# Attention with a running state, and a feed-forward layer: x transposed by TensorE in fp32 instead of in two fp16 parts by DMA

## The chip, the cores and the metric

The kernel runs on one core of a Trainium2 chip. Its time is the device time of one execution in microseconds (us); the median of the runs counts. A core has TensorE (PE; its weight loads are shown as PEld), VectorE (DVE), ScalarE (ACT), GpSimd (POOL), SyncE (SP, which here only issues DMAs) and 16 DMA engines. Each engine goes through its own list of instructions in order, and waits for the others by semaphores. SBUF is the memory of 128 partitions that they work on, PSUM the banks that TensorE writes.

## The reference

```python
x = L0_attn_x                                   # (4, 2048, 512) fp32
xn = _layernorm(x, axis=-1)                     # no gain or shift, eps 1e-5
# attention, 64 heads of width 8, heads(y): (4*64, 2048, 8)
q = heads(xn @ Wq.T + bq); k = heads(xn @ Wk.T + bk); v = heads(xn @ Wv.T + bv)
be = jnp.exp(beta)
q = jax.nn.softmax(be * q, axis=-1); k = jax.nn.softmax(be * k, axis=-1)
kv = jnp.cumsum(jnp.einsum('zsD,zsd->zsDd', k, v), axis=1)
kn = jnp.cumsum(k, axis=1)
num = jnp.einsum('zsD,zsDd->zsd', q, kv)
den = jnp.sum(q * kn, axis=-1, keepdims=True)
att = unheads(num / den) @ Wo.T + bo
# feed-forward: input rounded to fp8 (e4m3), clipped to +-448
x_q = jnp.clip(xn / input_scale, -448, 448).astype(jnp.float8_e4m3fn).astype(xn.dtype) * input_scale
ffn = jnp.einsum('bsi,oi->bso', x_q, weight_fp8 * weight_scale) + bias
return x + att + ffn
```

## The kernel before

The work goes in 64 steps. A step takes 32 tokens of each of the 4 sequences, 128 rows, one per partition. The cumulative sums are kept as a running state (st_run); inside a step the scores of q and k under a triangular mask (att) do the rest. Step i's tokens pass through the engines over several rounds of the loop: round i of `body` projects tokens i, does the attention of tokens i-1 and the output of tokens i-2, and gets x of tokens i+1 ready. Each engine has its own `body(i)`, written out by hand; that order is all that sets the order of the work. TensorE has its 64 rounds unrolled in the path that runs here (lines 1043 to 1045), the others loop over four.

fp32 accuracy of the projections comes from fp16 parts: every weight is held as w_hi + w_lo, and x as a high and a low part, so that `project` (L858) makes 12 matmuls of 512 columns for each of k, q and v. Before, the layer-normed x (xn, `normalise`, L597) is split in its natural layout, rows in partitions: ScalarE writes the high part (`high_input`, L450), GpSimd the low part (`low_input`, L388), and SP turns both with one DMA transpose into xT (`turn_x`, L311). ScalarE also scales xn into y. The rounding to fp8 is done by hand: VectorE makes from y's exponent a number y_magic (`magic`, L606), GpSimd adds and subtracts it (`rounding`, L396), VectorE clips (`quantise`, L617), and a second DMA transpose makes xq (`turn_xq`, L318). GpSimd also computes the reciprocal root of the variance by twelve small operations for two steps at once, in even rounds (`root`, L365).

TensorE's round is: k projection; scores and state of the first half (L888, L905); transpose of the attention output into the bank t_ps (L931); q projection; scores and state of the second half; feed-forward (L963); output projection (L872 to L876); q against the state (L985, 128 small matmuls that wait for masked_ready, stseqs_ready and qheads_ready); v projection; att against v (L1004, 128 small matmuls). masked_ready is given by VectorE's `mask_state` (L635; st_masked in the profile).

## Time and profile before

| | |
|---|---|
| median of 3 runs | 1386.97 us (1383.36 to 1387.37) |
| profiled execution | 1375.45 us, its span 1373.7 us |
| mean granted TensorE clock | 0.967 |
| TensorE busy | 1224.7 us, 89% |
| VectorE busy | 1024.7 us, 75% |
| ScalarE busy | 577.5 us, 42% |
| GpSimd busy | 321.5 us, 23% |
| DMA | 106.01 MB, 181142 packets; 120160 of them under 512 B |

Busy time is the time in which an instruction of the engine runs. The page's fourth part follows the work that ended last back to what released it: 86% of that chain is TensorE, 8% "issue", which is time in which the engine waited for nothing that the profile shows. In the rows below a matmul is named by what it writes and reads (vo_ps<-w_hi,al); "idle before" in brackets is how long its engine had nothing to do, and what ended that.

### The profile page before, as it was taken

The page shows a single profiled execution, that of the slowest core. Times are in us where ns is not written, and L with a number is a line of the kernel's source. Part 1 is how long each engine was busy: PE and PEld are TensorE (multiplying, and loading weights), DVE is VectorE, ACT ScalarE, POOL GpSimd, SP SyncE. Part 2 cuts the span into 40 slices and gives each one's busy share as a digit, 9 for nine tenths or more (in the row PEclk, how much of TensorE's full clock was granted, in tenths as well). Part 3 has the DMA queues.
Part 4 walks back from the last instruction along what each step waited for, and adds up shares of the span by engine and source line. Part 5 has one row for each costly group of instructions (what it writes and reads, how often), then busy time and mean ns, then how long its engine had stood idle before and what let it go on. Part 6 is the DMA issues. An engine that isn't in the chain of part 4 may idle for free.

```text
span 1373.7 us, 81313 instructions
## 1 busy us (share of the span) xinstructions
PE 1224.7 (89%) x36322; PEld 731.5 (53%) x36322; DVE 1024.7 (75%) x2031; ACT 577.5 (42%) x1049; POOL 321.5 (23%) x590
## 2 busy tenths in 40 slices
PE   1569999998999999999999899999999999999995
PEld 1335555555555555555555555555555555555653
DVE  4667778877777887778777777877777877778872
ACT  1534344444444444444444344344344444344431
POOL 3132222222222222222222222221222222122210
PEclk8789999999999999999999999999999999999998
DMA  8022232323323333333333333233233333323321
GB/s 223 10 67 65 75 84 75 82 76 79 75 73 83 70 85 76 81 74 85 76 75 77 76 80 71 77 79 69 76 86 66 76 86 77 75 77 76 69 65 42
DMA packets 181142, 106.01 MB, mean 77 GB/s; under 512 B 120160, under 2 KB 153056, under 8 KB 180832
## 3 DMA queue, kind: packets, MB, share of 16 engines
q1 hardware_dynamic: 180112, 99.79, 30.3%
q8 instruction: 289, 4.73, 1.5%
q10 hardware_dynamic: 720, 1.31, 0.6%
q14 instruction: 21, 0.17, 0.1%
HBM read 40.20 MB, written 16.78 MB: 41 GB/s over the span
## 4 chain that ended last, share of the span: by engine, by line
PE 86%; issue 8%; DVE 2%; DMA 1%; SPq 1%; POOL 0%; ACT 0%; POOLq 0%; DVEq 0%; ACTq 0%
PE s_ps L888 10%; PE a_ps L985 7%; PE a_ps L1004 6%; PE a_ps L905 6%; PE k_ps L861 5%; PE vo_ps L861 5%; PE vo_ps L963 5%; PE vo_ps L863 4%; PE k_ps L865 4%; PE vo_ps L865 4%; PE k_ps L863 4%; PE vo_ps L872 4%; PE vo_ps L874 4%; PE vo_ps L876 4%; PE q_ps L863 4%
## 5 line engine op out<-in xcount | busy, mean ns | idle before, releaser
L507 ACT ACTIVATE q_heads<-qT,cst 128x512 f32<-128x512 f32 x256 | 164.0, 711 | 88.1 <-DVE qT L753 88.1
L400 POOL TENSOR_TENSOR y_sum<-y,y_magic 128x512 f32<-128x512 f32 x64 | 81.4, 1272 | 450.3 <-DVE y_magic L614 450.3
L659 DVE TENSOR_TENSOR att<-s_ps,cst 128x512 f32<-128x512 f32 x256 | 163.8, 681 | 2.1 <-PE s_ps L888 2.1
L393 POOL TENSOR_TENSOR x_split<-xn,x_split 128x512 f16<-128x512 f32 x64 | 74.0, 1157 | 370.6 <-ACT x_split L455 363.4
L498 ACT ACTIVATE q_e<-q_shift,q_exp_scale 128x512 f32<-128x512 f32 x64 | 46.2, 722 | 252.0 <-DVE q_shift L632 252.0
L888 PE MATMUL s_ps<-q_heads,kT 32*32 32x128 f32 x8192 | 148.3, 272 | 2.1 <-issue 1.2
L888 PEld LDWEIGHTS s_ps<-q_heads,kT 32*32 32x32 f32 x8192 | 113.6, 103 | 56.3 <-issue 56.3
L985 PE MATMUL a_ps<-st_seqs,q_heads 128*32 128x36 f32 x8192 | 99.3, 201 | 35.6 <-issue 33.9
L712 DVE TENSOR_TENSOR vp<-vo_ps,vp 128x512 f32<-128x512 f32 x64 | 44.3, 692 | 109.1 <-PE vo_ps L865 109.1
L985 PEld LDWEIGHTS a_ps<-st_seqs,q_heads 128*32 128x32 f32 x8192 | 89.1, 109 | 68.4 <-issue 66.1
L905 PE MATMUL a_ps<-vp,k_e 32*32 32x36 f32 x8064 | 115.0, 198 | 6.4 <-issue 6.3
L861 PE MATMUL k_ps<-w_hi,xT 128*128 128x512 f16 x256 | 101.4, 396 | 19.0 <-DMA xT<-x_split 11.7
L863 PE MATMUL vo_ps<-w_lo,xT 128*128 128x512 f16 x256 | 102.0, 398 | 9.8 <-issue 9.8
L905 PEld LDWEIGHTS a_ps<-vp,k_e 32*32 32x32 f32 x8064 | 101.3, 103 | 11.5 <-issue 8.2
L470 ACT ACTIVATE vo_ps<-bias,out_up 128x512 f32<-128x512 f32 x64 | 44.3, 692 | 148.7 <-DVE vp L712 142.9
L455 ACT ACTIVATE x_split<-xn 128x512 f16<-128x512 f32 x64 | 40.3, 630 | 157.4 <-DVE xn L603 157.4
L1004 PE MATMUL a_ps<-v_groups,att 128*32 128x36 f32 x8192 | 89.3, 199 | 18.5 <-issue 14.9
L865 PE MATMUL k_ps<-w_hi,xT 128*128 128x512 f16 x256 | 100.2, 391 | 5.7 <-issue 5.6
L1004 PEld LDWEIGHTS a_ps<-v_groups,att 128*32 128x32 f32 x8192 | 79.6, 109 | 45.4 <-issue 45.1
L861 PE MATMUL vo_ps<-w_hi,xT 128*128 128x512 f16 x256 | 101.7, 397 | 0.0
L865 PE MATMUL vo_ps<-w_hi,xT 128*128 128x512 f16 x256 | 101.5, 396 | 0.0
L863 PE MATMUL k_ps<-w_lo,xT 128*128 128x512 f16 x256 | 100.4, 392 | 0.0
(136 smaller groups left out, 2450.4 us busy)
## 6 DMA issues: line engine op xcount, KB each, us to landing
v_groups<-vp SPq DMA_DIRECT2D x1024, 18.0 KB, 2.4
x_in<-L_attn_x SPq DMA_DIRECT2D x64, 256.0 KB
x_res<-L_attn_x SPq DMA_DIRECT2D x64, 256.0 KB
out<-o_sb SPq DMA_DIRECT2D x64, 256.0 KB
w_own<-L_attn_Wk SPq DMA_DIRECT2D x1, 1024.0 KB, 11.4
w_own<-L_attn_Wq SPq DMA_DIRECT2D x1, 1024.0 KB, 13.5
w_own<-L_attn_Wv SPq DMA_DIRECT2D x1, 1024.0 KB, 15.2
att<-L_ffn_weight_fp SPq DMA_DIRECT2D x1, 1024.0 KB, 16.9
```

Of the source, the lines that this page charges most:

```text
L393: gp.tensor_tensor(x_split[:, 1, :], xn[:, :], x_split[:, 0, :], ALU.subtract)\
L400: gp.tensor_tensor(y_sum[:, :], y[:, :], y_magic[:, :], ALU.add).then_inc(ysum_ready, 1)
L507: last = sc.activation(q_heads[:, i.parity, :, j, :], qT[:, :, :], ACT.Copy, scale=head_mask[:, j:j + 1])
L659: v.tensor_tensor(att[:, c, :, :, :].rearrange("p g j s -> p (g j) s"), s_ps[:, DM * (c % 2):DM * (c % 2 + 1)].rearrange("p (h s) -> p h s ...
L861: mm(bank[:, :], xT[:, t.parity, 0, c, :], w_hi[:, m, c, :], start=(c == 0 and not seeded), stop=False, skip_group_check=seeded)
L863: mm(bank[:, :], xT[:, t.parity, 0, c, :], w_lo[:, m, c, :], start=False, stop=False, skip_group_check=seeded)
L865: last = mm(bank[:, :], xT[:, t.parity, 1, c, :], w_hi[:, m, c, :], start=False, stop=(c == KC - 1), skip_group_check=seeded)
L888: last = mm(s_ps[TOK * gl:TOK * (gl + 1), DM * n + P * gq:DM * n + P * (gq + 1)], kT[rows, t.parity, GL * gq + gl, :], q_heads[rows, t.par ...
L905: last = mm(a_ps[rows, col:col + J * VW], k_e[rows, t.parity, TOK * g:TOK * (g + 1)], vp[rows, t.parity, v_head(g):v_head(g) + J, :], star ...
L963: last = mm(vo_ps[:, :], xq[:, t.slot, c, :], w_hi[:, MF, c, :], start=False, stop=False, skip_group_check=True)
L985: mm(a_ps[TOK * j:TOK * (j + 1), a_col(g):a_col(g) + GW], q_heads[:, t.parity, g, j, :], st_seqs[:, t.parity, g, :, :], start=(g % (G // 2 ...
L1004: last = mm(groups[TOK * j:TOK * (j + 1), b], att[:, b, gq, j, :], v_groups[:, t.parity, :, b, gq, j, :], start=False, stop=True, skip_gro ...
```

## The change

xn is turned as it is, in fp32: TensorE transposes its four 128x128 blocks into the bank t_ps (`input_transpose`). ScalarE then copies the high part out of PSUM as fp16, already transposed (xh), and the scaled y as well; VectorE subtracts to get the low part (xl). The rounding chain works on the transposed y, so `quantise` writes xq directly. Both DMA transposes are gone from SP, and the subtraction from GpSimd. t_ps is now shared by the transposed x and the transposed attention output, which adds waits between their writers and readers. The steps move: in ScalarE's round `high_input` stands behind q_heads instead of at the start, in VectorE's `low_input` and `magic` stand ahead of scale_values at the end, and GpSimd does `root` ahead of `rounding`.

In the diff, context that says nothing is left out.

```diff
@@ -170,9 +170,8 @@
         xn = sb("xn", [P, DM])
-        x_split = sb("x_split", [P, 2, DM], F16)
-        xT = sb("xT", [P, 2, 2, KC, P], F16)
-        xq_rows = sb("xq_rows", [P, DM], F16)
+        xh = sb("xh", [P, 2, KC, P], F16)
+        xl = sb("xl", [P, 2, KC, P], F16)
         y = sb("y", [P, DM])
@@ -308,26 +306,9 @@
-            def turn_x(t):
-                sp.wait_ge(xl_ready, (t + 1).n)
-                if t.after(2):
-                    sp.wait_ge(v_done, (t - 1).n)
-                sp.dma_start_transpose(xT[:, t.parity].rearrange("p h c s -> p (h c) s"),
-                                       x_split[:, :, :].rearrange("p h d -> p (h d)")).then_inc(x_turned, 16)
-
-            def turn_xq(t):
-                sp.wait_ge(xq_ready, (t + 1).n)
-                if t.after(SLOTS):
-                    sp.wait_ge(f_done, (t - SLOTS + 1).n)
-                sp.dma_start_transpose(xq[:, t.slot, :, :], xq_rows[:, :]).then_inc(xq_turned, 16)
-
             def body(i):
...
                     move_v(i - 1)
-                if (i + 1).exists():
-                    turn_x(i + 1)
-                if i.exists():
-                    turn_xq(i)
                 if (i + SLOTS).exists():
@@ -385,14 +365,6 @@
-            def low_input(t):
-
-                pool.wait_ge(xh_ready, (t + 1).n)
-                if t.after(1):
-                    pool.wait_ge(x_turned, t.n * 16)
-                gp.tensor_tensor(x_split[:, 1, :], xn[:, :], x_split[:, 0, :], ALU.subtract)\
-                    .then_inc(xl_ready, 1)
-
             def rounding(t):
@@ -405,16 +377,14 @@
             def body(i):
-                if (i + 1).exists():
-                    low_input(i + 1)
-                    rounding(i + 1)
                 if i.parity == 0 and (i + PAIR).exists():
                     root(i + PAIR)
+                if (i + 1).exists():
+                    rounding(i + 1)
...
             root(Step(0, 0))
-            low_input(Step(0, 0))
             rounding(Step(0, 0))
@@ -449,14 +419,14 @@
-                act.wait_ge(xn_ready, (t + 1).n)
-                if t.after(1):
-                    act.wait_ge(x_turned, t.n * 16)
-                sc.activation(x_split[:, 0, :], xn[:, :], ACT.Copy).then_inc(xh_ready, 1)
+                act.wait_ge(xT_done, (t + 1).n)
+                if t.after(2):
+                    act.wait_ge(v_done, (t - 1).n)
+                sc.activation(flat(xh[:, t.parity]), t_ps[:, :], ACT.Copy).then_inc(xh_ready, 1)
                 if t.after(1):
...
                     act.wait_ge(magic_ready, t.n)
-                sc.activation(y[:, :], xn[:, :], ACT.Copy, scale=in_inv[:, :]).then_inc(y_ready, 1)
+                sc.activation(y[:, :], t_ps[:, :], ACT.Copy, scale=in_inv[:, :]).then_inc(y_ready, 1)
@@ -469,8 +439,6 @@
                         .then_inc(oseed_ready, 1)
-                if (i + 1).exists():
-                    high_input(i + 1)
                 if i.exists():
@@ -507,6 +475,8 @@
                     last.then_inc(qheads_ready, 1)
+                if (i + 1).exists():
+                    high_input(i + 1)
                 t = i - 1
@@ -598,14 +568,21 @@
                 if t.after(1):
-                    dve.wait_ge(xl_ready, t.n)
-                    dve.wait_ge(y_ready, t.n)
+                    dve.wait_ge(xT_done, t.n)
                 v.tensor_scalar(xn[:, :], x_in[:, t.slot, :], mv[:, t.slot, 0:1],
...
+            def low_input(t):
+
+                dve.wait_ge(xh_ready, (t + 1).n)
+                dve.wait_ge(y_ready, (t + 1).n)
+                if t.after(2):
+                    dve.wait_ge(v_done, (t - 1).n)
+                v.tensor_tensor(flat(xl[:, t.parity]), t_ps[:, :], flat(xh[:, t.parity]), ALU.subtract)\
+                    .then_inc(xl_ready, 1)
+
             def magic(t):
...
-                dve.wait_ge(y_ready, (t + 1).n)
                 v.tensor_scalar(y_exp[:, :].bitcast(I32), y[:, :].bitcast(I32), EXPONENT, None,
@@ -617,9 +594,9 @@
                 dve.wait_ge(yround_ready, (t + 1).n)
-                if t.after(1):
-                    dve.wait_ge(xq_turned, t.n * 16)
-                v.tensor_scalar(xq_rows[:, :], y_round[:, :], FP8_MAX, -FP8_MAX, ALU.min, ALU.max)\
+                if t.after(SLOTS):
+                    dve.wait_ge(f_done, (t - SLOTS + 1).n)
+                v.tensor_scalar(flat(xq[:, t.slot]), y_round[:, :], FP8_MAX, -FP8_MAX, ALU.min, ALU.max)\
                     .then_inc(xq_ready, 1)
@@ -741,8 +718,6 @@
                     shift(i, q_ps, q_done, q_max, qmax_ready, q_shift, qshift_ready, qe_ready)
-                if (i + 1).exists():
-                    magic(i + 1)
                 if t.exists():
@@ -765,6 +740,9 @@
                     variances(i + PAIR)
+                if (i + 1).exists():
+                    low_input(i + 1)
+                    magic(i + 1)
                 if i.exists():
@@ -809,6 +787,7 @@
             largest(MQ)
+            low_input(Step(0, 0))
             magic(Step(0, 0))
@@ -858,11 +837,11 @@
                 for c in range(KC):
-                    mm(bank[:, :], xT[:, t.parity, 0, c, :], w_hi[:, m, c, :], start=(c == 0 and not seeded),
+                    mm(bank[:, :], xh[:, t.parity, c, :], w_hi[:, m, c, :], start=(c == 0 and not seeded),
                        stop=False, skip_group_check=seeded)
-                    mm(bank[:, :], xT[:, t.parity, 0, c, :], w_lo[:, m, c, :], start=False, stop=False,
+                    mm(bank[:, :], xh[:, t.parity, c, :], w_lo[:, m, c, :], start=False, stop=False,
                        skip_group_check=seeded)
-                    last = mm(bank[:, :], xT[:, t.parity, 1, c, :], w_hi[:, m, c, :], start=False,
+                    last = mm(bank[:, :], xl[:, t.parity, c, :], w_hi[:, m, c, :], start=False,
                               stop=(c == KC - 1), skip_group_check=seeded)
@@ -889,6 +868,13 @@
                 last.then_inc(scores_done, 1)
+
+            def input_transpose(t):
+
+                pe.wait_ge(xn_ready, (t + 1).n)
+                for c in range(KC):
+                    last = transpose(t_ps[:, P * c:P * (c + 1)], xn[:, P * c:P * (c + 1)], ident)
+                last.then_inc(xT_done, 1)
@@ -908,7 +894,8 @@
                 if i.exists():
-                    pe.wait_ge(x_turned, (i + 1).n * 16)
+                    pe.wait_ge(xh_ready, (i + 1).n)
+                    pe.wait_ge(xl_ready, (i + 1).n)
                     pe.wait_ge(kseed_ready, (i + 1).n)
@@ -923,16 +910,15 @@
                     pe.wait_ge(an_ready, (t + 1).n)
-                    if t.after(1):
-                        pe.wait_ge(al_ready, t.n)
-                    else:
-                        pe.wait_ge(bvl_ready, 1)
+                    if i.exists():
+                        pe.wait_ge(y_ready, (i + 1).n)
                     for b in range(SEQS):
...
                     pe.wait_ge(bias_ready, 3)
+                    pe.wait_ge(y_ready, (i + 1).n)
                     for j in range(J):
@@ -957,7 +943,7 @@
                 if t.exists():
-                    pe.wait_ge(xq_turned, (t + 1).n * 16)
+                    pe.wait_ge(xq_ready, (t + 1).n)
                     pe.wait_ge(oseed_ready, (t + 1).n)
@@ -971,6 +957,13 @@
                     project_out(rest=True).then_inc(o_done, 1)
+                if (i + 1).exists():
+                    if fold:
+                        pe.wait_ge(bvl_ready, 1)
+                    else:
+                        pe.wait_ge(xl_ready, (i + 1).n)
+                        pe.wait_ge(y_ready, (i + 1).n)
+                    input_transpose(i + 1)
                 t = i - 1
@@ -1029,6 +1022,7 @@
             pe.wait_ge(c_loaded, 16)
+            input_transpose(Step(0, 0))
             for m in (MK, MQ, MV):
...
             pe.wait_ge(wl_ready, qkv_chunks)
```

TensorE, before, in the middle of the run: the end of the output projection, then L985 (a_ps<-st_seqs,q_heads), then v.

```order
L872 MATMUL vo_ps<-w_hi,ah 128x512
L874 MATMUL vo_ps<-w_lo,ah 128x512
L876 MATMUL vo_ps<-w_hi,al 128x512
L985 MATMUL a_ps<-st_seqs,q_heads 32x36 [waits stseqs_ready,masked_ready,qheads_ready]
L985 MATMUL a_ps<-st_seqs,q_heads 32x36 x63
```

The same place in the changed kernel, whose line numbers are lower (L855 was L876, L978 was L985).

```order
L851 MATMUL vo_ps<-w_hi,ah 128x512
L853 MATMUL vo_ps<-w_lo,ah 128x512
L855 MATMUL vo_ps<-w_hi,al 128x512
L876 MATMUL t_ps<-cst,xn 128x128 [waits xn_ready,y_ready,xl_ready]
L876 MATMUL t_ps<-cst,xn 128x128 x3
L978 MATMUL a_ps<-st_seqs,q_heads 32x36 [waits stseqs_ready,masked_ready,qheads_ready]
L978 MATMUL a_ps<-st_seqs,q_heads 32x36 x63
```

Four transposes of xn stand between the output projection and L985.

GpSimd, before, in an even round: rounding, then root, whose first three operations stand here.

```order
L393 TENSOR_TENSOR x_split<-xn,x_split 128x512 [waits x_turned,xh_ready]
L400 TENSOR_TENSOR y_sum<-y,y_magic 128x512 [waits magic_ready,y_ready]
L404 TENSOR_TENSOR y_round<-y_sum,y_magic 128x512 [waits xq_ready,ysum_ready]
L378 TENSOR_TENSOR newton<-guess 128x2 [waits xn_ready,guess_ready]
L380 TENSOR_TENSOR newton<-newton,minus_half 128x2 [waits newton_steps]
L382 TENSOR_TENSOR newton<-newton,three_halves 128x2 [waits newton_steps]
```

In the changed kernel, the end of root and what follows it in the same round.

```order
L358 TENSOR_TENSOR newton<-newton 128x2 [waits newton_steps]
L360 TENSOR_TENSOR newton<-newton,minus_half 128x2 [waits newton_steps]
L362 TENSOR_TENSOR newton<-newton,three_halves 128x2 [waits newton_steps]
L364 TENSOR_TENSOR rstd<-newton 128x2 [waits newton_steps]
L372 TENSOR_TENSOR y_sum<-y,y_magic 128x512 [waits magic_ready,y_ready]
L376 TENSOR_TENSOR y_round<-y_sum,y_magic 128x512 [waits xq_ready,ysum_ready]
```

The subtraction is gone, and y_sum and y_round stand behind root. On VectorE two pieces move; the changed kernel's end of a round shows where they now are.

```order
L547 BN_STATS stats<-x_in 128x6 [waits x_loaded0]
L548 REGISTER_ALU
L550 BN_AGGR mv<-stats 128x2 [waits stats_ready]
L577 REGISTER_ALU [waits mv_ready]
L581 TENSOR_TENSOR xl<-t_ps,xh 128x512 [waits v_done,y_ready,xh_ready]
L586 TENSOR_SCALAR y_exp<-y 128x512
L591 TENSOR_SCALAR y_magic<-y_exp 128x512 [waits yround_ready,yexp_ready]
L689 TENSOR_TENSOR vp<-vo_ps,vp 128x64x8 [waits krec_ready,v_done]
```

Before, vp followed the statistics directly, and y_exp and y_magic stood between q_shift and the second pair of masks.

## Rows read from the trace of the kernel before

**Rows 1.** Page, section 1: busy us, share, instructions

```profile
PE 1224.7 (89%) x36322; PEld 731.5 (53%) x36322; DVE 1024.7 (75%) x2031; ACT 577.5 (42%) x1049; POOL 321.5 (23%) x590
```

**Rows 2.** List of waits of TensorE: us in total, times, longest us

```profile
PE a_ps L985 <- issue: 33.9, 40, 2.9
...
PE a_ps L1004 <- issue: 14.9, 13, 2.5
...
PE k_ps L861 <- DMA xT<-x_split: 11.7, 1, 11.7
```

**Rows 3.** Two steps: stretch, us; PE, PEld, DVE, ACT, POOL busy; clock; DMA share; GB/s

```profile
699.30:718.00 18.70, 18.39 (x569) 11.12 (x570) 15.77 (x33) 8.62 (x17) 5.03 (x10) 1.00 0.28 70
718.00:739.20 21.20, 18.92 (x570) 11.38 (x570) 15.37 (x29) 8.99 (x17) 4.72 (x9) 1.00 0.37 88
```

**Rows 4.** Chain of waits of step A, and its last L876 in the timeline

```profile
712.15 0.30 issue
712.45 1.61 PE a_ps L985 x110
...
711.77 0.38 PE L876 MATMUL vo_ps<-w_hi,al 128*128 128x512 f16 x1
```

**Rows 5.** Chain of waits, step B

```profile
732.64 1.85 issue
```

**Rows 6.** Timeline of VectorE, step A: start us, us, instruction

```profile
709.32 0.42 DVE L609 TENSOR_SCALAR y_exp<-y 128x512 int32<-128x512 int32 x1
...
710.11 1.28 DVE L659 TENSOR_TENSOR att<-s_ps,cst 128x512 f32<-128x512 f32 x2
...
711.93 0.42 DVE L639 TENSOR_TENSOR st_masked<-a_ps,cst 128x288 f32<-128x288 f32 x1
...
716.80 0.69 DVE L712 TENSOR_TENSOR vp<-vo_ps,vp 128x512 f32<-128x512 f32 x1 [0.75 <-PE vo_ps L865]
```

**Rows 7.** Timeline of GpSimd, step A

```profile
711.68 1.28 POOL L404 TENSOR_TENSOR y_round<-y_sum,y_magic 128x512 f32<-128x512 f32 x1
...
719.22 0.20 POOL L384 TENSOR_TENSOR rstd<-newton 128x2 f32<-128x2 f32 x1
```

**Rows 8.** Timeline of all engines, step B

```profile
720.74 0.69 DVE L628 TENSOR_REDUCE k_max<-k_ps 128x64 f32<-128x512 f32 x1 [0.41 <-PE k_ps L865]
...
729.29 1.26 SPq L315 DMA_TRANSPOSE xT<-x_split  x1
...
730.35 0.42 DVE L639 TENSOR_TENSOR st_masked<-a_ps,cst 128x288 f32<-128x288 f32 x1
...
730.64 1.22 SPq L322 DMA_TRANSPOSE xq<-xq_rows  x1
...
731.06 0.38 PE L876 MATMUL vo_ps<-w_hi,al 128*128 128x512 f16 x1
...
731.37 1.27 PE L985 MATMUL a_ps<-st_seqs,q_heads 128*32 128x36 f32 x105
```

**Rows 9.** Timeline of TensorE in the setup

```profile
57.47 0.38 PE L865 MATMUL q_ps<-w_hi,xT 128*128 128x512 f16 x1
57.69 1.04 PE L1024 MATMUL s_ps<-cst,att 128*128 128x128 f32 x8
58.56 1.04 PE L1024 MATMUL a_ps<-cst,att 128*128 128x128 f32 x8
```

**Rows 10.** Page, section 3: packets, MB, share of 16 engines

```profile
q8 instruction: 289, 4.73, 1.5%
```

**Rows 11.** Page, section 5, a copy of ScalarE

```profile
L470 ACT ACTIVATE vo_ps<-bias,out_up 128x512 f32<-128x512 f32 x64 | 44.3, 692 | 148.7 <-DVE vp L712 142.9
```

**Rows 12.** Timeline, setup, ahead of step 1

```profile
70.69 2.56 ACT L507 ACTIVATE q_heads<-qT,cst 128x512 f32<-128x512 f32 x4 [0.29 <-DVE qT L753]
...
78.49 0.61 PE L861 MATMUL k_ps<-w_hi,xT 128*128 128x512 f16 x1 [11.72 <-DMA xT<-x_split]
```

**Rows 13.** Timeline of VectorE, setup

```profile
20.90 0.43 DVE L614 TENSOR_SCALAR y_magic<-y_exp 128x512 f32<-128x512 f32 x1
```

4 lines of the change are left out of this document (1 added, 3 removed).

## The prediction

> **What bounds the kernel now.** I read the page first, for the engines' shares. TensorE is busy 89% of the span and VectorE 75% [rows 1], and the list of waits has TensorE waiting for the transposed x only once, 11.7 us in the setup [rows 2]. Everything else it lost is called "issue" there: 33.9 us in 40 places ahead of L985, the first being the largest group [rows 2]. So the time is a sum over 64 steps of what TensorE does in a step, plus those gaps.
>
> Next I cut two neighbouring steps out of the middle, step A from 699.30 and step B from 718.00 [rows 3]. They do the same work, at full granted clock (1.00), in 18.70 and 21.20 us. TensorE is busy 18.39 us in A: it is full. VectorE has 2.9 us to spare (15.77 busy), ScalarE and GpSimd more than half. The whole run is alternately like A and like B.
>
> The chain of waits says what the gaps are, and there are two kinds. In A, 0.30 us lie between the last output projection matmul and L985 [rows 4]. L985 needs masked_ready, and the VectorE operation that gives it, st_masked, runs from 711.93 for 0.42 us, to 712.35; L985 starts at 712.45 [rows 6]. That is a real wait for VectorE, though the profile calls it issue. The spacing shows it too: from the start of the last L876 to the start of L985 it is 712.45 - 711.77 = 0.68 us in A, and 731.37 - 731.06 = 0.31 us in B, where st_masked was over at 730.77 [rows 8]. (The last L876 of A starts at 711.77 [rows 4].) In B the gap is another: 1.85 us in the middle of a run of identical L985 matmuls that wait for no semaphore [rows 5]. TensorE's program is 2 x 36322 instructions [rows 1], the instruction queue moved 4.73 MB in 289 packets [rows 10], 16 KB or some 250 instructions each. L985 is 128 matmuls with their weight loads, 256 instructions in 1.6 us. I take such gaps for TensorE waiting for its next packet of code. About one comes in two steps.
>
> **The change, part by part.**
>
> TensorE gets four fp32 transposes of 128x128 in each step, between L876 and L985 (with one wait on xl_ready, y_ready and xn_ready, all given much earlier: the first two belong to the step in hand, whose projections have run, and xn is written at the step's start). Nearest rows: eight weight transposes start at 57.69 and the next eight at 58.56, so 0.109 us each, 0.43 us for four; and they follow a 512-column matmul by 0.22 us (57.47 to 57.69) [rows 9]. Then comes L985, which starts 0.31 us after whatever fp16 matmul precedes it, 0.09 us more than 0.22. So L876 to L985 becomes 0.22 + 0.43 + 0.09 = 0.74 us. Bounds: 0.43 us more per step than the free spacing of 0.31 if the switch to 32-column tiles costs the same behind them; 0.8 us more if a transpose's full duration of about 0.27 us must drain once more ahead of L985. I take 0.43, the row's. The Trainium skill, "TensorE: Matmul & The Clock Gate", Part 4, gives about 275 ns for a transpose in a kernel's context, and says that transposes don't count as busy for the clock. With that price four would be 1.1 us and 64 steps 70 us. The rows' starts say 0.11 us each when they are issued back to back, and the granted clock is 1.00 through both steps, which hold four such transposes already [rows 3], so I don't use it.
>
> In steps like A the insertion falls on the wait for st_masked. VectorE loses the magic pair from ahead of it: y_exp at 709.32 to the next operation at 710.11 is 0.79 us [rows 6], so st_masked ends some 0.8 us sooner at 711.56 (q_e on ScalarE starts when q_shift is over, about 709.4, takes some 0.7 us [rows 11] and is needed at 710.5: it doesn't hold it). TensorE is then free of it, and L985 starts at 711.77 + 0.74 = 712.51 instead of 712.45: 0.06 us for the step. The wait was paying for it already.
>
> In steps like B the 0.43 us are added in full, and GpSimd adds something. Its order becomes root, then rounding. Root runs in even steps only (A is one), behind variances, and ends at 719.42 [rows 7]; before, rounding was over long before (y_round ended at 712.96). Now magic stands at the end of VectorE's step, behind low_input, and GpSimd starts y_sum only when root is done: 719.45, and with 1.3 us for each of the pair (y_round took 1.28 [rows 7]) y_round ends at about 722.05. quantise of step B waits for that in VectorE's order ahead of k_max, and adds 0.4 us: k_max at 722.4 instead of 720.74 [rows 8], 1.7 us late. Behind it in the order are the whole shift of k, two masks, key sums, the shift of q; minus 0.79 for the magic pair st_masked is 0.9 us later, at 731.67 instead of 730.77, L985 at 731.75. TensorE alone would come to 731.06 + 0.74 = 731.80. So in B it just fits: 0.43. In those odd steps in which L985 already follows st_masked at once, it costs the 0.9 in full. In the middle 60 steps L985 follows st_masked within 0.1 us in about 40 (counted through the timeline, as the pair at 712.35 and 712.45), some 13 of them odd. Mean of an odd step: (18 x 0.43 + 13 x 0.9) / 31 = 0.63 us.
>
> VectorE gets low_input, a subtraction from PSUM like the 0.69 us of L712 [rows 6], and magic's 0.79, between variances and scale_values. There it had 0.75 us of idle time before L712 [rows 6]; vp comes about 0.75 us later. Behind it wait vo's seed, the moves of v (16 DMAs that have a whole step) and state of the next step, which is 3.5 us behind the step's start: covered. xl itself: q_heads takes 2.56 us [rows 12] from 711.25, xh and y each about 0.7 [rows 11] to 715.2, low_input is over by 716.8, and the next projection of k starts at 718.0: 1.2 us of slack, about the same in B less half a microsecond. st_seqs, now behind xh and y on ScalarE, is 0.6 us later and is used a step later. Cost 0; if that cover goes, up to 0.7 us a step. GpSimd loses its subtraction, ScalarE reads PSUM instead of SBUF: nothing on the path.
>
> The two DMA transposes of a step go. TensorE waited for them only once, so this gives nothing directly; SP reaches load_x 2.5 us sooner (1.26 and 1.22 us of issue [rows 8]), which nothing waits for. Their packets share the DMA engines with the packets of code. I can't price that from one trace: 0, with -0.3 us for each of some 31 code gaps (-10 us) as an end, and +5 us if the loads moved into that place press as much.
>
> Setup. Step 1's projection waited for xT until 78.49 [rows 12]. Now: q_heads from 70.69 for 2.56, xh and y to 74.7, low_input to 75.4: k starts at 75.5, 3.0 us sooner. Against that, the chain of the setup passes magic(0), which ended at 21.33 [rows 13] and now stands behind the transposes, two copies and low_input: about 22.5, 1.1 us later. Together -1.9 us.
>
> Code gaps. A step's instructions for TensorE grow by 8 matmul halves and a few waits, about 1%, so some 0.3 gap more, under 1 us; where the packet's end falls in a step shifts faster than before (two steps were nearly a whole number of packets), which can move the sum of the gaps either way. About 31 gaps near 2 us are 62 us; a quarter of that, 15 us, is my range for it, and 0 the value. The Trainium skill, "Runtime: NRT & Kernel Launch", Instruction fetch mechanics, has the 16 KiB blocks of 256 instructions and calls the crossing mostly hidden; this trace agrees on the size and shows it not hidden in dense stretches [rows 5].
>
> **Sum.** 31 steps like A x 0.06 = 2; 31 like B x 0.63 = 20; setup -2; code gaps and DMA 0: +20 us. Against the profiled execution that is 1375.45 + 20 = 1395.5 (its span 1373.7 and 1.75 around it). That execution was 11.5 us below the median of the runs, 1386.97, and the runs go from 1383.36 to 1387.37; on the median's scale the forecast is 1407 us.
>
> **Rivals.**
> 1. VectorE and GpSimd become the bound in every step: low_input and magic sit between statistics and scale_values, quantise waits for y_round also in even steps, and TensorE waits both ahead of L985 and ahead of k. For it: L985 already follows st_masked in 40 steps. Against: 2.9 us idle in A [rows 3]. Price 0.7 us in every step instead of 0.33 on average: 62 x 0.7 = 43, and with 0.8 us for the insertion 50: 1387 + 45 = 1432.
> 2. The insertion hides altogether: a code gap that follows in L985 starts from the same packet request, so 0.43 us put in ahead of it shorten the gap by as much (in B the gap at 732.64 [rows 5] would come 1.3 us behind the four transposes). If that holds for 15 to 25 of the 31, the sum falls to about 20 - 10 - 2 = 8 us or, with the cheaper DMA side, to about 0: 1387 to 1391.
> 3. Faster: code packets are late because the transposes' packets are in the way. They are issued at 729.29 and 730.64 in step B [rows 8], and the gap comes right after, at 732.64. If that is what makes half of the 62 us, 31 us go: 1387 + 20 - 31 = 1376. It decides from about 20 us on, a third of the gaps. Against: the same gaps stand ahead of L1004 too, 14.9 us in 13 places [rows 2], five microseconds further on in the step.
>
> **Chances.** Forecast (slower by 10 to 32 us) 0.50, rival 1 0.17, rival 2 0.15, rival 3 0.18. A difference under 0.3%, 4 us, can't be told from none here. Slower: 0.50 + 0.17 + a quarter of rival 2 = 0.71; same: most of rival 2 and a little of 3, 0.13; faster 0.16. Range: from 1384, the upper edge of rival 3, to 1433, rival 1. The likeliest case's own range is 1397 to 1419.
>
> **What would show it.** Right: L876 to L985 about 0.74 us in A-like steps, with st_masked over before; transposes of xn 0.11 us apart; k's first matmul never waiting for xl; k_max some 1.7 us later in odd steps only; no wait at step 1's projection beyond 75.5. Wrong: "PE k_ps <- DVE xl" in the waits; TensorE's issue gaps summing to much under 60 us (rival 3) or falling where the transposes stand (rival 2); L985 behind st_masked in nearly all steps (rival 1).

## The result, and the profile after

The changed kernel takes 1390.96 us (median of 18 runs, 1387.32 to 1401.68), the kernel before, run on the same chip between them, 1382.82 (18 runs, 1378.26 to 1398.11). The ratio is 1.0055, 95% interval 1.0029 to 1.0080: slower by 8 us. Forecast were +20 us (+1.4%), so the direction is right and the size less than half.

The profiled executions say more than that, 1375.45 before and 1394.16 after, 18.7 us apart. One execution stands several microseconds off the median of its kernel (here 7 below and 3 above). Verdicts below therefore go by ratios of medians to the kernel before in the same job; the traces are read for where time stands.

Page of the kernel after, sections 1 and 3:

```profile
PE 1241.1 (89%) x36578; PEld 753.9 (54%) x36578; DVE 1095.4 (79%) x2095; ACT 563.4 (40%) x1049; POOL 259.0 (19%) x526
...
DMA packets 78741, 80.83 MB, mean 58 GB/s; under 512 B 17760, under 2 KB 50656, under 8 KB 78432
...
q1 hardware_dynamic: 77712, 74.61, 18.7%
q8 instruction: 291, 4.77, 1.5%
```

TensorE has 256 matmuls more than in [rows 1] and 16 us more busy time, VectorE 71 us more, GpSimd 63 less. 25 MB of DMA are gone. The list of waits, against [rows 2]:

```profile
PE a_ps L978 <- issue: 36.3, 30, 3.0
...
DVE xq L599 <- POOL y_round L376: 32.1, 28, 1.2
...
PE a_ps L997 <- issue: 10.5, 13, 2.3
```

L978 is L985 of before, L997 is L1004. New is the second row: the quantise waits for GpSimd's rounding in 28 steps, all odd. One odd step, the timelines of GpSimd, VectorE and TensorE:

```profile
1053.66 1.27 POOL L376 TENSOR_TENSOR y_round<-y_sum,y_magic 128x512 f32<-128x512 f32 x1 [0.16 <-POOL y_sum L372]
...
1054.97 0.43 DVE L599 TENSOR_SCALAR xq<-y_round 128x512 f16<-128x512 f32 x1 [1.18 <-POOL y_round L376]
1055.31 0.68 DVE L605 TENSOR_REDUCE k_max<-k_ps 128x64 f32<-128x512 f32 x1
...
1064.13 0.42 DVE L616 TENSOR_TENSOR st_masked<-a_ps,cst 128x288 f32<-128x288 f32 x1
...
1063.01 0.38 PE L855 MATMUL vo_ps<-w_hi,al 128*128 128x512 f16 x1
1063.22 0.60 PE L876 MATMUL t_ps<-cst,xn 128*128 128x128 f32 x4
1064.65 1.30 PE L978 MATMUL a_ps<-st_seqs,q_heads 128*32 128x36 f32 x128 [0.83 <-issue]
```

The reader is to see a delay travel. y_round ends at 1054.9, the quantise starts then, k_max behind it, and nine microseconds later st_masked is over at 1064.55. L978 starts at 1064.65, 1.64 us after the last L855, where TensorE alone would need 0.75. In another odd step VectorE is early, L978 doesn't wait, and it starts 0.75 us after the last L855:

```profile
705.29 0.38 PE L855 MATMUL vo_ps<-w_hi,al 128*128 128x512 f16 x1
705.51 0.60 PE L876 MATMUL t_ps<-cst,xn 128*128 128x128 f32 x4
706.04 1.14 PE L978 MATMUL a_ps<-st_seqs,q_heads 128*32 128x36 f32 x110
```

Measured from the starts of the weight loads, in steps 3 to 60, the stretch from the first matmul of the output projection (L872 to L876, now L851 to L855) to L978 takes 3.37 us in even steps (3.22 before) and 3.80 in odd ones (2.94 before). L978's run itself became shorter (L985 before is the first row, L978 the second; busy, mean ns, idle before):

```profile
L985 PE MATMUL a_ps<-st_seqs,q_heads 128*32 128x36 f32 x8192 | 99.3, 201 | 35.6 <-issue 33.9 <-DVE st_masked L639 0.7
```

```profile
L978 PE MATMUL a_ps<-st_seqs,q_heads 128*32 128x36 f32 x8192 | 88.2, 201 | 37.4 <-issue 36.3 <-DVE st_masked L616 1.1
```

The same matmuls keep TensorE busy for 88.2 us in place of 99.3. The 128 of a step, a run from here on, take 1.24 us (median) in place of 1.56: some 46 halts of 0.1 to 0.2 us inside the runs of steps 2 to 60 are gone (6.8 us), and the mean spacing from one matmul to the next is 8.6 ns in place of 9.2. The second group of the same shape and number, v's, didn't change:

```profile
L1004 PE MATMUL a_ps<-v_groups,att 128*32 128x36 f32 x8192 | 89.3, 199 | 18.5 <-issue 14.9 <-DMA v_groups<-vp 3.1
```

```profile
L997 PE MATMUL a_ps<-v_groups,att 128*32 128x36 f32 x8192 | 89.3, 200 | 14.5 <-issue 10.5 <-DMA v_groups<-vp 3.9
```

TensorE's long waits for code stayed: 57 with 86.1 us before, 63 with 85.7 after (steps 2 to 60, over 0.3 us each). They are stops in which TensorE's stream of instructions stands still without a semaphore, and in both traces nearly all end at an instruction whose number, counted along TensorE's program, is 193 or 194 modulo 256. On them rival 3 stood, and it is out.

### The profile page after: what moved, and what is told of

The parts are those of the page before. It is cut to its first block, busy times and chain, and to the rows that moved or that the text cites. A ratio compares the mean times of both kernels' runs of the same rounds, so it can differ in the third digit from the quotient of the medians.

```text
span 1392.3 us, 81649 instructions
## 1 busy us (share of the span) xinstructions
PE 1241.1 (89%) x36578; PEld 753.9 (54%) x36578; DVE 1095.4 (79%) x2095; ACT 563.4 (40%) x1049; POOL 259.0 (19%) x526
## 3 DMA queue, kind: packets, MB, share of 16 engines
q1 hardware_dynamic: 77712, 74.61, 18.7%
## 4 chain that ended last, share of the span: by engine, by line
PE 79%; issue 10%; DVE 4%; POOL 3%; SPq 1%; DMA 1%; ACT 1%; POOLq 0%; DVEq 0%; ACTq 0%
PE s_ps L867 9%; PE a_ps L891 6%; PE a_ps L997 5%; PE a_ps L978 5%; PE vo_ps L949 5%; PE vo_ps L840 4%; PE k_ps L840 4%; PE vo_ps L851 4%; PE vo_ps L853 4%; PE vo_ps L855 4%; PE vo_ps L842 4%; PE vo_ps L844 4%; PE k_ps L844 4%; PE k_ps L842 4%; PE q_ps L842 4%
## 5 line engine op out<-in xcount | busy, mean ns | idle before, releaser
L447 ACT ACTIVATE k_e<-k_shift,k_exp_scale 128x512 f32<-128x512 f32 x64 | 46.2, 722 | 318.2 <-DVE k_shift L609 300.2
L978 PE MATMUL a_ps<-st_seqs,q_heads 128*32 128x36 f32 x8192 | 88.2, 201 | 37.4 <-issue 36.3
L840 PE MATMUL k_ps<-w_hi,xh 128*128 128x512 f16 x256 | 100.4, 392 | 16.2 <-issue 12.0
L978 PEld LDWEIGHTS a_ps<-st_seqs,q_heads 128*32 128x32 f32 x8192 | 79.2, 109 | 51.3 <-issue 51.1
L997 PEld LDWEIGHTS a_ps<-v_groups,att 128*32 128x32 f32 x8192 | 80.1, 110 | 43.9 <-issue 43.7
L997 PE MATMUL a_ps<-v_groups,att 128*32 128x36 f32 x8192 | 89.3, 200 | 14.5 <-issue 10.5
L844 PE MATMUL vo_ps<-w_hi,xl 128*128 128x512 f16 x256 | 100.3, 392 | 2.0 <-issue 2.0
L842 PE MATMUL vo_ps<-w_lo,xh 128*128 128x512 f16 x256 | 100.4, 392 | 1.8 <-issue 1.8
L840 PE MATMUL vo_ps<-w_hi,xh 128*128 128x512 f16 x256 | 101.0, 395 | 0.8 <-issue 0.8
L844 PE MATMUL k_ps<-w_hi,xl 128*128 128x512 f16 x256 | 99.8, 390 | 2.0 <-issue 2.0
L842 PE MATMUL k_ps<-w_lo,xh 128*128 128x512 f16 x256 | 99.8, 390 | 1.3 <-issue 1.2
L853 PE MATMUL vo_ps<-w_lo,ah 128*128 128x512 f16 x260 | 99.6, 383 | 1.4 <-issue 1.4
```

The lines of the kernel that those rows point to most:

```text
L840: mm(bank[:, :], xh[:, t.parity, c, :], w_hi[:, m, c, :], start=(c == 0 and not seeded), stop=False, skip_group_check=seeded)
L842: mm(bank[:, :], xh[:, t.parity, c, :], w_lo[:, m, c, :], start=False, stop=False, skip_group_check=seeded)
L844: last = mm(bank[:, :], xl[:, t.parity, c, :], w_hi[:, m, c, :], start=False, stop=(c == KC - 1), skip_group_check=seeded)
L853: mm(vo_ps[:, :], ah[:, j, :], w_lo[:, MO, j, :], start=False, stop=False, skip_group_check=rest)
L978: mm(a_ps[TOK * j:TOK * (j + 1), a_col(g):a_col(g) + GW], q_heads[:, t.parity, g, j, :], st_seqs[:, t.parity, g, :, :], start=(g % (G // 2 ...
L997: last = mm(groups[TOK * j:TOK * (j + 1), b], att[:, b, gq, j, :], v_groups[:, t.parity, :, b, gq, j, :], start=False, stop=True, skip_gro ...
```

## The experiments

All were timed in five rounds. Ratios are to the kernel before in the same job, with their 95% interval; for two kernels of different jobs I divide their ratios, which is good to 0.4 to 0.6%, 5 to 9 us.

**One part of the change at a time.** In the kernel after, the quantise was moved behind the shift of q:

```
-                    if i.after(1):
-                        quantise(i)
                     shift(i, k_ps, k_done, ...)
...
                     shift(i, q_ps, q_done, ...)
+                    if i.after(1):
+                        quantise(i)
```

> The changed kernel with one move on VectorE: quantise(i), the clip that waits for GpSimd's y_round, stands behind the shift of q instead of ahead of the shift of k. In the changed kernel's profile TensorE spends 1.13 us between the first transpose of xn and L978 in odd steps and 0.74 us in even ones, and VectorE waits 32 us for y_round in 28 places. Theory 1 (the late y_round is a real part of the loss, as forecast): that extra 0.4 us goes in some 31 odd steps, 12 us, and the time falls from about 1391 to about 1379, below the kernel before (1383). Theory 2 (code gaps behind L978 take back what the wait costs): the 0.4 us goes ahead of L978 and comes back as longer gaps in L978 and L997, and the time falls by 5 us at most.

1374.05 us, 0.9941 (0.9912 to 0.9969), 16 us (1.1%) below the kernel after and faster than the kernel before. That is theory 1, a little beyond its 1379. The piece from the first transpose to L978 is 0.74 us in all steps (1.13 in odd ones before the move), the stretch from the output projection on is 0.43 us shorter in odd steps, 13 us in all, and the wait for y_round is gone:

```profile
DVE xq L599 <- POOL y_round L376: 0.6, 1, 0.6
```

Next two DMA transposes of a tile that nobody reads stood where SP had turn_x and turn_xq:

```
+                    sp.dma_start_transpose(d_xT[:, :, :], d_src[:, 0:2 * DM])
+                    sp.dma_start_transpose(d_xq[:, :, :], d_src[:, 2 * DM:])
```

> The changed kernel with two DMA transposes per step put back on SP where they were (128x1024 and 128x512 fp16, from a constant tile into tiles that nothing reads). If the transposes' packets delay TensorE's packets of code, the time rises by some 10 us (0.3 us for each of about 31 gaps), to 1401, and the gaps in L978, L840 and L997 are longer; if they press on nothing, it stays within 3 us of 1391.

1404.43 us, 1.0144 (1.0102 to 1.0186), 12 us above the kernel after. The size is the one that the expectation gave to late packets of code, but the waits for code hardly grew (87.6 us in place of 85.7). What is back is L985's long busy time:

```profile
L992 PE MATMUL a_ps<-st_seqs,q_heads 128*32 128x36 f32 x8192 | 98.3, 202 | 34.4 <-issue 33.2 <-DVE st_masked L630 1.2
```

Then the kernel before with TensorE's new work and none of the rest (first; VectorE's normalise also waits for these transposes, two steps later), and with nine empty increments in its place (second), about as many instructions a step (1157 and 1158):

```
+                    for c in range(KC):
+                        last = transpose(t_ps[:, P*c:P*(c+1)], xn[:, P*c:P*(c+1)], ident)
...                                                  # the second:
+                for _ in range(9):
+                    pe.sem_inc(pe_pad, 1)
```

> The kernel before with the four fp32 transposes of xn into t_ps between the output projection and L985 in each step, read by nobody; the DMA transposes and all else stay. Theory 1 (the insertion costs 0.43 us in odd steps and 0.06 in even ones): +15 us, from 1383 to 1398. Theory 2 (a code gap behind it shrinks by as much): less than half of it, +3 to +8 us.

> The kernel before with nine more semaphore increments on TensorE in each step, ahead of L985, so that a step has 1158 instructions, as in the changed kernel, instead of 1149. They have no work. If only the sum of code matters: +1%, under 1 us, the time stays at 1383. If the place at which the 256-instruction blocks end within a step matters, the code gaps fall in other places (L872, L905, L931 as often as L985) and their sum moves, by up to 15 us either way.

1393.72 us, 1.0069 (1.0043 to 1.0094), and 1374.90, 0.9946 (0.9918 to 0.9974). The first, some 9 us above the kernel before, lies between its two theories. Nine instructions that do nothing made the kernel 7 us faster; against them the transposes' own price is 1.0124, 17 us (forecast 15 without the late quantise). The traces agree: the stretch from the output projection to q against the state grew by 0.12 us in even and 0.41 in odd steps over the kernel before, 16 us.

**Transposes or bytes.** Plain copies of the same bytes, then of 4 KB each, in the place of the dummy transposes:

```
-                    sp.dma_start_transpose(d_xT[:, :, :], d_src[:, 0:2 * DM])
+                    sp.dma_start(d_xT[:, :], d_src[:, 0:2 * DM])          # then [0:16, 0:P]
```

> The changed kernel with two plain DMA copies of the same bytes (128 rows of 2 KB and 128 rows of 1 KB, SBUF to SBUF, not read by anything) in the places on SP where the two dummy DMA transposes of the earlier experiment stood. With the dummy transposes the kernel took 1404.4 us, without them 1391.0, and the run of L978 had a median of about 1.5 us beside 1.24. Theory A: what slows TensorE's small fp32 matmuls is the transposing transfer itself, its many small packets (about 100,000 of them in the whole kernel), not bytes moved and not SP's time: 1391 to 1394 us, median of L978's run 1.24 to 1.28 us, few or none of the halts of 0.12 to 0.19 us in it. Rival B: bytes on the DMA rings or SP's issuing delay what stands behind (x_in, v_groups, the code's packets): 1400 to 1406 us, with L978's run as long as with the dummy transposes.

> The changed kernel with two plain DMA copies of 16 rows of 256 bytes each (4 KB in place of 256 KB and 128 KB) in the places on SP where the two copies and, before, the two dummy DMA transposes stood; SP issues and waits as there. With the large copies the kernel took 1400.0 us, with the dummy transposes 1404.4, with neither 1391.0. Theory A (bytes on the DMA engines): what these transfers cost goes with the bytes, so 1390 to 1393 us. Rival B (SP's time: each issue delays the loads and the moves of v behind it): as with the large copies, 1399 to 1404 us.

1399.98 us, 1.0135 (1.0093 to 1.0178), and 1389.49, 1.0091 (1.0056 to 1.0126). Theory A of the first expectation fell: copies cost as much as transposes, within the noise. The small ones cost 5 us, 6 less than the large, and the intervals touch on both sides, so their time doesn't settle bytes against SP's issues. The busy time of the run does say something: 93.3 us with the large copies and 94.6 with those of 4 KB, halfway both times. It doesn't go by bytes.

Last, the kernel before without its own DMA transposes from step 2 (x) and 4 (xq) on:

```
+                if t.n < 2:
                     sp.dma_start_transpose(xT..., x_split...).then_inc(x_turned, 16)
+                else:
+                    sp.sem_inc(x_turned, 16)
```

> The kernel before with its own two DMA transposes a step left out from step 2 (x) and step 4 (xq) on: SP waits as before and raises the semaphores itself, TensorE multiplies the x of the first steps again, so the kernel leaves out the moving of x. Instructions a step on TensorE are the same (1149). Theory A: the transfers cost about what putting them back into the changed kernel cost, 11 to 14 us, mostly by their bytes: 1366 to 1372 us beside 1380 for the kernel before. Rival B (the prediction's step: they cost nothing, and the dummy ones only disturbed a kernel whose VectorE was later): 1377 to 1383 us.

1381.40 us, 0.9958 (0.9929 to 0.9988), 6 us faster (2 to 10) than the kernel before, which took 1388.67 in this job: between the two theories. L985 (L991 here) has its short run:

```profile
L991 PE MATMUL a_ps<-st_seqs,q_heads 128*32 128x36 f32 x8192 | 89.4, 201 | 34.7 <-issue 33.2 <-DVE st_masked L645 0.7
```

**What stretches the runs, from the kept traces.** Take every run of L978 (L985) in steps 2 to 60 of all twenty kernels, measured from its first to its last weight load without stops of over 0.2 us, and sort it by what SP issued from 0.9 us before its start to 1.0 us after it:

```
                                              runs   mean us   over 1.15 us
neither of the two below                       651      1.10             43
a DMA transpose of x, or a dummy of it         204      1.27            191
the kernel's own load of x                     224      1.21            114
both                                           101      1.31             95
```

Before, 53 of the 59 runs had one of them near; in the kernel after, 2 of 59. With the 4 KB dummies 35 runs have the load of x near, alone (20 runs, 1.18 us) or with a dummy (15, 1.38); the other 24 take 1.10. The late quantise has no dummies, and its 11 runs with the load of x near take 1.23 us against 1.08 for the rest. So the transposes seem to stretch the run in two ways: when they are issued at it, and by standing ahead of the load of x in SP's list, so that it falls there. The load is issued 1.1 us behind the start of the run before and 2.1 us ahead of it after (medians). That fits L1004 and L997 too: of 1160 runs of theirs six had such a transfer near, and those took 1.33 to 1.72 us, where the means are 1.09 to 1.13. This is a comparison of steps; no run moved the load of x by itself.

**GpSimd's order.** First the kernel before with the magic pair at the end of the round and the quantise late, GpSimd's order untouched; then the kernel after with GpSimd's old order, whose edit stands here:

```
+                if (i + 1).exists():
+                    rounding(i + 1)
                 if i.parity == 0 and (i + PAIR).exists():
                     root(i + PAIR)
-                if (i + 1).exists():
-                    rounding(i + 1)
```

> The kernel before with one part of the change alone: VectorE's magic pair of step i+1 stands behind the variances at the end of its round, no longer ahead of the masks of the scores, and the quantise of it behind the shift of q of the next round, so that it waits for nothing. The DMA transposes stay. Theory A: in the steps in which L985 waits for st_masked (the even ones of the traces), 0.79 us of VectorE's work is gone from ahead of it, and TensorE gains up to 0.2 to 0.3 us in each: 1376 to 1380 us beside 1382 of the kernel before. Rival B: the pair only moves to where VectorE is late as well (ahead of vp, and so of the state of the next step): 1382 to 1388 us.

> The changed kernel with GpSimd's order as before: the rounding of step i+1 ahead of the Newton steps of the next pair's root, in place of behind them. In the changed kernel the root comes first in every second step and the quantise, ahead of the shift of q, waits for the rounding (DVE xq L599 <- POOL y_round, 32.1 us in 28 waits). Theory A: the early rounding frees the quantise but the root is then late behind it, and the normalise of step i+1 waits for the root at the head of VectorE's round (in the kernel before with the late magic, 97.8 us in 27 waits, +47 us in all): 1395 to 1430 us. Rival B: only the quantise is freed: 1374 to 1380 us.

1424.91 us, 1.0320 (1.0274 to 1.0366), and 1427.71, 1.0288 (1.0240 to 1.0336). In the first neither theory had it; the second was expected. With magic late, a rounding that stands ahead of the root holds it, and the normalise waits at the head of VectorE's round (kernel after with the old order):

```profile
DVE xn L572 <- POOL rstd L364: 109.8, 30, 5.4
```

In the kernel after that wait is 10.3 us, in the first experiment 97.8. Root first, a part of the change, is worth 2.3% there.

**Where the code waits fall.** Three increments a step make 1152 instructions, four and a half times 256, so that the waits return to the same places; increments ahead of step 0 choose them.

```
+                for _ in range(3):
+                    pe.sem_inc(pe_pad, 1)
...
+            for _ in range(36):                     # then 76
+                pe.sem_inc(pe_pad, 1)
```

> The kernel before with three semaphore increments a step on TensorE ahead of L985 (1152 instructions a step, four and a half times 256, in place of 1149), and 36 more ahead of step 0, so that TensorE's long waits for code, which in every trace so far end at an instruction whose number is 193 or 194 modulo 256, fall at the same places in every second step: some 40 instructions into an even step and 168 into an odd one (q behind the k part, and so on every 256). In the traces so far pairs of steps whose waits fell there took 37.3 to 39.5 us, against a mean of 40.2. Theory A: the place where these waits fall decides how much of them is hidden; it is locked at a good place: 1335 to 1365 us, with pairs of steps at 38 to 39.5 us throughout. Rival B: the pattern was chance, and the nine increments of the earlier experiment gained their 9 us otherwise: 1373 to 1386 us, like the kernel before.

> The same three increments a step and 76 ahead of step 0 in place of 36: the waits for code fall at instruction 0 to 5 and 128 to 133 of a step. Pairs of steps with the waits there took 40.5 to 43.8 us in the traces so far. Theory A (the place decides): 1400 to 1440 us, 50 or more above the kernel with 36. Rival B (chance): within 8 us of the kernel with 36.

1389.19 us, 1.0081 (1.0052 to 1.0110), and 1366.18, 0.9898 (0.9861 to 0.9935). The place matters by 1.8%, but my choice of the good one, from pairs of steps in other traces, was the wrong way round, and neither time lies where a theory had it. In the good one the waits stand in k's projection, where little else waits (58.2 us); in the bad one in L988:

```profile
PE a_ps L988 <- issue: 55.5, 33, 2.8
```

Then I left out waits of TensorE that others imply, in the kernel with the late quantise: five a step, then eight with 58 increments ahead of step 0, the latter also with the early quantise (ahead of the shift of k, as in the kernel after). One of them:

```
-                    pe.wait_ge(xh_ready, (i + 1).n)
                     pe.wait_ge(xl_ready, (i + 1).n)
```

> The changed kernel with the quantise behind the shift of q (1374.05 us so far) and five of TensorE's waits a step left out that other waits already imply (xh at k, y at the transposes of a and of xn, xl at the latter, ah at the output projection), some 1153 instructions a step in place of 1158. Theory A: an empty instruction costs next to nothing (about 0.06 us each where TensorE is behind its queue), and the number a step counts only by where the waits for code fall: 1360 to 1385 us, and what it gives is read from the pairs of steps. Rival B: fewer instructions are a straight gain of 5 x 0.06 us x 64 = 19 us: 1355 us.

> The candidate for the best version: the changed kernel with the quantise behind the shift of q, eight of TensorE's waits a step left out that other waits imply, which should make 1152 instructions a step (four and a half times 256), and 58 increments ahead of step 0, so that its long waits for code fall at instruction 5 or so of an even step and 133 of an odd one, where they did in the variant of the kernel before that took 1366.2 us (1389.2 with the waits 40 instructions later). Theory A: the place decides here too, and adds to what the late quantise gave: 1345 to 1365 us. Rival B: the place was good only beside the DMA transposes: 1370 to 1380 us, like the unlocked version (1375.9).

> The same as the candidate, but with the quantise where the changed kernel has it, ahead of the shift of q: the late quantise is the one difference, with the waits for code at the same places. Theory A: the late quantise costs what it cost without the lock, 17 us: 12 to 22 us above the candidate. Rival B: part of the 17 us was where the waits for code happened to fall: under 8 us above it.

1375.94 us, 0.9988 (0.9962 to 1.0014), 1393.61, 1.0117 (1.0072 to 1.0162), and 1412.99, 1.0238 (1.0191 to 1.0285). Five waits fewer gained nothing (a ratio of 1.0047 to the late quantise with all of them, inside the noise), and the second missed both its theories, 1345 to 1365 and 1370 to 1380 us. There the count came to 1153 in place of 1152, so the places drifted by one a step; the waits for code sum to 80.6 and 88.6 us. The late quantise is worth 1.2% in this pair, 17 us by the ratios and 19 by the medians.

**One wait more.** Without the ninth, qheads_ready ahead of L978, which scores has already waited for:

```
-                    pe.wait_ge(qheads_ready, (t + 1).n)
                     if i.exists():
                         pe.wait_ge(masked_ready, (t + 1).n * 2)
```

> The changed kernel (early quantise) with nine of TensorE's waits a step left out that other waits imply, 1152 instructions a step, its waits for code held at the places of the variant of the kernel before that took 1366.2 us (0.9898 of the kernel before). The pair of them is the change with its waits for code at the same places. Theory A (insertion +19, quantise +17 to 19, transfers gone -12, setup -2): 20 to 26 us above 1366, 1386 to 1392 us. Rival B: the place that was good for the kernel before is a bad one for the changed order: 1400 us or more (the kernel with 1153 instructions a step took 1413.0).

> The candidate for the best version: late quantise, 1152 instructions a step, and waits for code held at instruction 160 of an even step and 32 of an odd one. Over the traces of the three kernels with the late quantise, pairs of steps with the waits there took 39.2 to 39.3 us, those with them at 208 to 240 took 40.9, the mean 40.2. Theory A: held there the kernel keeps the 39.3: 1374 - 30 x 0.9 = 1347, so 1340 to 1362 us. Rival B: what a pair gains there is given back in the next when all stand there, since an engine that had run ahead has no lead left: 1368 to 1380 us.

1348.38 us, 0.9720 (0.9683 to 0.9756), 38 us below what either theory had, and with the late quantise and 159 increments 1352.66, 0.9758 (0.9712 to 0.9803), as theory A had it. Against 1412.99 the first has the same count, 1153, the same places to within one, and waits for code of 37.6 us instead of 88.6. So it wasn't the place. Next that one wait alone, and all nine with the late quantise:

> The changed kernel with one redundant wait left out, TensorE's wait for qheads_ready ahead of L978 (scores has waited for the same value earlier in the step). That wait is one of the nine left out in the variant that took 1348.4 us and the only one that the variant with 1413.0 us still had; in their traces both have 1153 instructions a step, numbered the same to within one, and differ in the long waits for code (88.6 us in 51 against 37.6 us in 41, and TensorE at the lower clock for 65 against 15 us). Theory A: that wait itself decides how far TensorE's code is fetched ahead of L978: 1340 to 1370 us here. Rival B: it decides nothing; whether the long waits come depends on how all engines fall together, and a small edit throws it one way or the other: 1380 to 1400 us, near 1391.

> The variant that took 1348.4 us with the quantise behind the shift of q: late against early quantise once more, now where few long waits for code come. Theory A: the late quantise gives 17 to 20 us as in the two pairs measured so far, and the waits stay few: 1325 to 1335 us. Rival B: its gain is the mechanism's 13 to 28 us, but the long waits for code come back as in the variant with 1393.6 us (80.6 us of them): 1365 to 1395 us.

1355.82 us, 0.9800 (0.9771 to 0.9829): the kernel after gains 35 us, 2.5%, by one wait that says nothing new. The list of waits, L977 being L978:

```profile
PEld a_ps L977 <- DVE st_masked L616: 19.4, 21, 1.1
...
PE a_ps L977 <- DVE st_masked L616: 14.2, 20, 0.8
...
PEld a_ps L977 <- issue: 9.5, 47, 0.9
```

Of the 36.3 us of issue ahead of L978's matmuls 1.1 are left, and the wait for st_masked now bears its name. Waits for code inside this run (stops of over 0.19 us) went from 24.1 us in 13 places to 1.9 in 4.

The count of waits isn't all that changed. Leaving qheads_ready out takes no instruction away: both kernels have 1158 a step. In the kernel after, as in every kernel with the three waits, one instruction ahead of L978 waits for stseqs_ready and masked_ready, and the first weight load of L978 itself for qheads_ready, given long before. With two, the instruction ahead waits for stseqs_ready alone, and the weight load for masked_ready, the late one. L978 then starts at the least 0.054 us after st_masked is over, in place of 0.10. So a rival stands that no run tests: that it matters on which instruction the late wait sits, and not how many waits there are. Three waits with masked_ready on the weight load would tell.

The last kernel takes 1319.88 us, 0.9542 (0.9513 to 0.9571), the fastest of all and some 5 us below its theory A. The late quantise is worth 1.8% there, 25 us by the ratios (28 by the medians, of two jobs); the stretch ahead of the run is 0.80 us shorter in odd steps, 25 us. Its waits for code sum to 35.1 us.

```profile
PE 1224.7 (93%) x36578; PEld 754.8 (57%) x36578; DVE 1094.8 (83%) x2095; ACT 560.5 (42%) x1049; POOL 258.4 (20%) x526
```

## Why the prediction was right in direction and wrong in size

The forecast was 20 us and 8 were measured. One term was too small by 10 us, and one was put at nothing that is worth 6 to 12 us the other way; the rest of the difference isn't shown.

**The insertion: right.** Forecast were 0.74 us from the last output projection matmul to L978, and the free steps have 0.75, 0.44 more than before. Even steps grew by 0.15 us (forecast 0.06). TensorE's new work alone costs 17 us (forecast 15).

**The late quantise: right mechanism, sized too low.** I gave it 0.9 in place of 0.43 us in 13 odd steps. It was 14 of 29, but some 1.3 us each (1.64 in place of 0.31 in the step shown), so that a mean odd step cost 0.86 in place of 0.63. Taking the wait away gained 16, 17 to 19 and 25 to 28 us in three pairs, where the sum had 6.

**The step that failed: "this gives nothing directly", the DMA transposes at 0.** I looked for who waits for them, found one wait in the setup, wrote that SP reaches the load of x 2.5 us sooner "which nothing waits for", and priced the rest only by the packets of code. The runs showed in its place that L985's matmuls take longer with these transfers: 99.3 us busy with them, 88.2 and 89.4 without, 98.3 when put back. By the comparison of steps they do it when they are issued at the run, and by keeping the load of x there. Taking them from the kernel before gave 6 us, putting them into the kernel after cost 12. My end of -10 was of the right size by luck, from another mechanism: the waits for code didn't move (86.1 and 85.7 us), as rival 3 needed.

**Code gaps at 0, within 15: inside the range.** I had taken them for 31 gaps of 2 us, 62 us; they were 57 with 86.1 us, but their sum didn't change. Nine empty instructions gave -7 us. The kernel after has nine more instructions as well; whether they gave it the same 7 isn't shown.

**The sum again.** 17 for the insertion, 16 for the quantise, -6 to -12 for the transfers, -7 for the count: 14 to 20 us, against 8 measured. The -7 is carried over from another kernel, unproven here. The remaining -6 to -12 stay open: 2 of them are the setup (step 1's k starts at 76.5 in place of 78.5, forecast -1.9), and each term is good to some 5 us, so the rest may be no more than their errors. The magic pair, now out of st_masked's way, may be in it; the experiment made for it measured GpSimd's order instead. The profiled pair, 18.7 apart, would have called the forecast exact; the medians don't.

**The rivals.** Rival 1: VectorE holds L978 in 14 steps, not in nearly all. Rival 2: the sum of the code gaps is unchanged, so the insertion didn't hide in them, although its 8 us are what was measured. That is luck, and its sum was wrong besides: it takes off the setup's 2 us, which the 20 already hold, and 1387 + 8 is 1395, not 1391. Rival 3 would have had the gaps fall by 31 us.

## What to carry to other kernels

Price a transfer that nobody waits for by what it does to the engines while it runs, and by what it pushes back in its queue: compare the busy time of one group of small matmuls in steps with and without a transfer near it. When an operation ends later on one engine, look for whoever waits for it early in its own fixed order, and move that wait back too; here a line moved on VectorE was worth more than the whole change. And ahead of a dense run of small matmuls try leaving out a wait that earlier waits imply, and look on which instruction the late wait then sits. Elsewhere, five such waits left out gave nothing.

## What the runs showed of the hardware

TensorE's waits for code end at the same instruction numbers modulo 256 in all traces (193 or 194, nearly all of them), but sum to anything from 35 to 118 us in kernels that do the same work. With three semaphore waits ahead of L978 the waits for code inside its run sum to 19 to 60 us in fifteen kernels (24.1 in the kernel after), and to nothing in the sixteenth, where they are held at k's projection; with two waits, in four kernels, to 0 to 6 us (1.9 with that one edit). Why isn't settled: the traces show which instruction waits, not when its code was asked for.

With the wait for st_masked in an instruction of its own, L978 starts 0.10 us after st_masked is over at the earliest (kernel after); with that wait on its first weight load, 0.054 us (1355.82 and 1348.38 us).

In the pair of 1412.99 and 1348.38 us the granted clock is at 1.2 GHz for 65 us behind the setup with the ninth wait, and for 15 without it; the rest is at 2.4. Fewer such stretches and a shorter time don't always go together: the late quantise has more of them than the kernel after (67 and 56 us, from step 1 on), and is 16 us faster.

A run of 128 fp32 matmuls of 128x36 takes longer when SP issues a transfer of x within a microsecond of its start, though the transfer touches none of its operands: 1.10 us without, 1.27 with a DMA transpose or a dummy, 1.21 with a load of x from HBM (means over twenty kernels). Dummies of 4 KB went with as long a busy time as copies of 384 KB (94.6 and 93.3 us, 88.2 without).
